# The second mixture's weights: loaded in the attention's last part instead of in the second routing

## The chip, the cores and the metric

One core of a Trainium2 chip runs the whole kernel. The metric is the device time of one execution in microseconds (us); lower is better. Fine effects are read in the profile of one execution, whose clock starts at its first instruction. The engines are named as in the profile: PE (TensorE, matrix products), PEld (its weight loads), DVE (VectorE), ACT (ScalarE), POOL (GpSimd), SP (SyncE, which here only issues DMAs).

## The reference

A sequence of 2048 tokens with 128 channels goes through three residual steps: a mixture of experts with half weight, an attention block, and the same mixture again, with the same weights.

```
x = x + 0.5 * mixture(layernorm(x))
x = x + attention_block(layernorm(x))
x = x + 0.5 * mixture(layernorm(x))
```

The mixture has eight experts, and each token goes to the two with the largest gate probability:

```
probs = softmax(x @ gate_W);  rw, sel = top_k(probs, 2);  rw = rw / rw.sum()
mlp_out = gelu(x @ mlp_W1 + b1) @ mlp_W2 + b2                 # experts 0 to 3, hidden 512
h0 = layernorm(x) * g0 + b0;   basis0 = 1 - tanh((h0 - grid) / 2)**2      # experts 4 to 7
z  = basis0 @ kan_W0 + c0      # 128 channels x 8 grid points -> 256
h1 = layernorm(z) * g1 + b1;   basis1 = 1 - tanh((h1 - grid) / 2)**2
kan_out = basis1 @ kan_W1 + c1 # 256 x 8 -> 128
out = sum over the two chosen experts of rw * expert_out
```

The attention block has 16 heads of 8 channels, a window of the 128 tokens before each one, and a gated feed-forward part with 352 hidden channels.

## The kernel before, in words

The kernel is written without a scheduler: every engine has its own list of instructions, and semaphores tie the lists together. A stage is a `nc.Block`; all five engines meet at a barrier at its end. The stages follow each other as

1. first routing (`route`, n = 0), 0 to 44 us,
2. first mixture (`moe_blocks`), to about 225 us, then the weighted sums into `xs`,
3. attention: `project`, `attend`, and `finish_attention` (the output product, the second layer norm and the feed-forward part), the last of them from 392 to 442 us,
4. second routing (`route`, n = 1), 442 to about 476 us,
5. second mixture (`moe_blocks`), to the end at 671.8 us.

**Routing.** VectorE normalizes the 16 tiles of 128 tokens (L307), TensorE transposes them (L496) and multiplies by the gate (L508). VectorE finds the two largest logits, counts the tokens of each expert, and builds tables that say for every block of 128 places which token rows it takes (L327 to L433). SP stores the normalized rows to memory in HBM (`x_rows`, L454) and a second copy of them, rescaled on ScalarE for the KAN experts (L534, store L457). At the end GpSimd gathers the rows of the first blocks with indirect DMAs (L477): `m_x_in` of the first MLP block, `k_x_in` of the first KAN block, `m_x_in` of the second MLP block. They wait for both stores (`rows_in_dram`) and for the tables (`rows_ready`).

**Mixture.** The number of blocks of each expert is known only at run time, so the engines read counts and expert numbers from tables into registers (L631, L558) and loop. TensorE begins with the transpositions of the first MLP block (L807) and the first KAN block (L829), then multiplies the MLP block by its expert's first weights (L813), which ScalarE has copied into `m_w1` (L1129). The first KAN product comes some blocks later (L835) and waits for all KAN weights.

**Weights.** `moe_weights` (L138) takes memory for one mixture's weights: 2 MB for both layers of the MLP experts, 0.25 MB for their biases, 8 MB for the KAN experts. In the kernel before it is called by `moe` for each mixture anew, and the memory is given back after the mixture; the attention lies in the same place. So SP loads the same weights twice, each time inside the routing: `load_mlps` (L163) and `load_kan` (L170), in one queue with the two stores of the rows. [...] In `finish_attention` SP has nothing to do.

Of the kernel before, what the change touches and what calls it, by code (L numbers as in the profile page):

```python
# [29 lines left out]
E2 = NE // 2  # L30
# [107 lines left out]
def moe_weights(nc, k, ctx, n):  # L138

    sb = lambda name, shape, dt=F32: ctx.enter_context(nc.sbuf_tensor(f"{name}_{n}", shape, dt))  # L140
    k.m_x_in = [sb(f"m_x_in{u}", [P, C]) for u in range(2)]
    k.k_x_in = sb("k_x_in", [P, C])
    k.rows_first = sb("k_rows_first", [P, 3, 1], I32)
    k.m_loaded = [k.sem(f"m_loaded{u}_{n}") for u in range(2)]
    k.k_loaded = k.sem(f"k_loaded_{n}")
    k.kan_w0 = sb("kan_w0", [P, E2, G, F2])
    k.kan_w1 = sb("kan_w1", [P, E2, F2C, G, C])
    k.mlp_w1 = sb("mlp_w1", [P, E2, F])
    k.mlp_w2 = sb("mlp_w2", [P, E2, FC, C])
    k.mlp_b2 = sb("mlp_b2", [P, E2, C])  # L150


def load_shared(q, k, a):

    q.dma_start(k.kan_ln[:], a.kan_ln).then_inc(k.small_loaded, 16)
    q.dma_start(k.kan_b0[:], a.kan_sl_b0.partition_broadcast(P)).then_inc(k.small_loaded, 16)
    q.dma_start(k.kan_b1[:], a.kan_sl_b1.partition_broadcast(P)).then_inc(k.small_loaded, 16)
# [5 lines left out]
def load_mlps(q, k, a, n):  # L163
    q.dma_start(k.mlp_w1[:], a.mlp_W1.rearrange("e p f -> p e f")).then_inc(k.mlp_loaded[n], 16)
    for e in range(E2):
        q.dma_start(k.mlp_w2[:, e], a.mlp_W2[e].rearrange("(c p) h -> p c h", p=P)).then_inc(k.mlp_loaded[n], 16)
    q.dma_start(k.mlp_b2[:], a.mlp_b2.partition_broadcast(P)).then_inc(k.mlp_loaded[n], 16)


def load_kan(q, k, a, n, e):  # L170
    q.dma_start(k.kan_w0[:, e], a.kan_sl_W0[e].rearrange("(p g) o -> p g o", g=G)
                ).then_inc(k.kans_loaded_again if n else k.kan_loaded[e], 16)
    q.dma_start(k.kan_w1[:, e], a.kan_sl_W1[e].rearrange("(c p g) o -> p c g o", p=P, g=G)
                ).then_inc(k.kans_loaded_again if n else k.kan_loaded[e], 16)
# [32 lines left out]
def route(nc, k, a, n, s):  # L207
# [6 lines left out]
    with ExitStack() as ctx:  # L214
# [13 lines left out]
        first = sb("first", [P, TOPK, NT])  # L228
# [51 lines left out]
        with nc.Block(no_gpsimd_drain=True) as block:  # L280
# [156 lines left out]
            @block.sync  # L437
            def _(sp):
                if n == 0:
                    x_tiles = a.x[0].rearrange("(t p) c -> p t c", p=P)  # L440
                    for g in range(NT // PART):
                        part = slice(g * PART, (g + 1) * PART)
                        sp.dma_start(k.xs[:, part], x_tiles[:, part]).then_inc(k.x_loaded[g], 16)
                    sp.dma_start(k.gate_w[:], a.gate_W).then_inc(k.gate_loaded, 16)
                    b1_rows = a.mlp_b1.rearrange("e (c p) -> (e c) p", p=P)
                    sp.dma_start(b1_rows_sb[:], b1_rows).then_inc(k.b1_loaded, 16)
                load_mlps(sp, k, a, n)
                if n == 0:
                    load_shared(sp, k, a)
                load_kan(sp, k, a, n, 0)  # L450

                rows = k.x_rows.rearrange("(h t p) c -> h p t c", h=2, p=P)
                sp.wait_ge(xn_ready, NT)
                sp.dma_start(rows[0], xn).then_inc(k.rows_in_dram[n], 16)  # L454
                load_kan(sp, k, a, n, 1)
                sp.wait_ge(xh_ready, NT)
                sp.dma_start(rows[1], xh).then_inc(k.rows_in_dram[n], 16)  # L457
                load_kan(sp, k, a, n, 2)
                load_kan(sp, k, a, n, 3)

            @block.gpsimd
            def _(pool):
# [752 lines left out]
                    sp.wait_ge(k.stored_out, 16 * (NT // PART))  # L1215


def moe(nc, k, a, n, s, out=None):

    with ExitStack() as ctx:  # L1220
        moe_weights(nc, k, ctx, n)
        route(nc, k, a, n, s)
        moe_blocks(nc, k, a, n, s, out)

NH = 16
HD = C // NH
PAIRS = NH // 2
# [475 lines left out]
def finish_attention(nc, k, a, s):  # L1703

    with ExitStack() as ctx:
# [28 lines left out]
        with nc.Block(no_gpsimd_drain=True) as block:  # L1734
            @block.tensor
            def _(pe):
# [28 lines left out]
                def by_w2(g):  # L1765
                    pe.wait_ge(hid_ready, 3 * g + 3)
                    if g < 2:
                        pe.wait_ge(h_ready, NCH)
                    else:
                        pe.wait_ge(x_ready, g - 1)  # L1770
                    for t in range(4):
                        for c, (at, size) in enumerate(HIDC):
                            last = nc.tensor.matmul(w_ps[g % 2][:, t], hid[g % 2][0:size, c, t * P:(t + 1) * P],
                                                    s.w2[0:size, c], start=(c == 0), stop=(c == 2))
                    last.then_inc(y_done, 1)
# [12 lines left out]
                    by_w2(g - 1)  # L1788
                by_w2(NCH - 1)

            @block.scalar
            def _(act):
                def affine(g):
                    act.wait_ge(nT_done, g + 1)
                    if g >= 2:
                        act.wait_ge(u_done, 3 * (g - 1))
                    nc.scalar.activation(n2T[g % 2][:], T_ps[g % 2][:], ACT.Identity, bias=s.ln_vec[:, 3:4],
                                         scale=s.ln_vec[:, 2:3]).then_inc(nT_ready, 1)

                act.preload_act_table(ACT.Silu)  # L1800
                def silu(g, c):
                    size = HIDC[c][1]
                    act.wait_ge(u_done, 3 * g + c + 1)
                    if g:
                        act.wait_ge(hid_ready, 3 * g + c - 2)
                    nc.scalar.activation(gate[0:size, c], u1_ps[(3 * g + c) % 2][0:size],
                                         ACT.Silu).then_inc(silu_done, 1)

                affine(0)
                silu(0, 0)  # L1810
                silu(0, 1)
                affine(1)
                silu(0, 2)
                for g in range(1, NCH):
                    if g + 1 < NCH:
                        affine(g + 1)
                    for c in range(3):
                        silu(g, c)
# [121 lines left out]
    return s  # L1940


def attention(nc, k, a, s):
    with ExitStack() as ctx:
        sb = lambda name, shape, dt=F32: ctx.enter_context(nc.sbuf_tensor(f"s_{name}", shape, dt))
        s.res = sb("res", [P, NT, C])
        s.mask_set = k.sem("mask_set")
        s.attT = sb("attT", [P, T])
        with ExitStack() as stacks:
            sb2 = lambda name, shape, dt=F32: stacks.enter_context(nc.sbuf_tensor(f"s_{name}", shape, dt))  # L1950
            s.qT = sb2("qT", [P, T + P])
            s.kT = sb2("kT", [P, T])
            s.q_bd = sb2("q_bd", [P, NB, HG, QB])
            s.k_bd = sb2("k_bd", [P, NB, HG, QB])
            s.v_bd = sb2("v_bd", [P, NB, NG, HG * HD])
            s.m_rows = sb2("m_rows", [P, T + P], BF16)
            s.mask = sb2("mask", [P, 2, P], BF16)
            s.no_keys = sb2("no_keys", [P, WINDOW], BF16)
            s.v_heads = sb2("v_heads", [P, NB, NG, HD])
            project(nc, k, a, s)  # L1960
            attend(nc, k, a, s)
        finish_attention(nc, k, a, s)

def macaron(nc, a, out):
    with ExitStack() as ctx:
        k = Names()
        k.sb = lambda name, shape, dt=F32: ctx.enter_context(nc.sbuf_tensor(name, shape, dt))
        k.sem = lambda name: ctx.enter_context(nc.semaphore(name))
        k.moe_sems = {}

        def moe_sem(name):
            if name not in k.moe_sems:
                k.moe_sems[name] = k.sem(name)
            return k.moe_sems[name]

        k.moe_sem = moe_sem
        k.x_rows = nc.dram_tensor("x_rows", [2 * T, C], F32, kind="Internal").ap()
        k.y_rows = nc.dram_tensor("y_rows", [ROWS_OUT, C], F32, kind="Internal").ap()
        k.xs = k.sb("xs", [P, NT, C])

        k.st = k.sb("st", [P, NT, 6])
        k.mv = k.sb("mv", [P, NT, 2])
        k.var_eps = k.sb("var_eps", [P, NT])
        k.rstd = k.sb("rstd", [P, NT])
        k.got = k.sb("got", [P, TOPK, NT, C])
        constants(nc, k)
        moe_tensors(nc, k)
        with ExitStack() as weights:
            s = attention_weights(nc, k, weights)
            moe(nc, k, a, 0, s)  # L1990
            attention(nc, k, a, s)
        moe(nc, k, a, 1, None, out)


# [40 lines left out]
```

## Time and profile before

| | |
|---|---|
| device time, median of 3 runs | 672.86 us (672.86 to 674.57) |
| the profiled execution | 673.61 us, its span 671.8 us |
| TensorE busy | 539.7 us, 80% of the span |
| VectorE busy | 450.6 us, 67% |
| ScalarE busy | 373.9 us, 56% |
| GpSimd busy | 263.3 us, 39% |
| mean granted TensorE clock | 0.903 |
| DMA | 46.51 MB, mean 69 GB/s |

The busy shares are means over stages of different kinds. TensorE's share says that it is the busiest, not that it sets the end everywhere. The chain of waits, followed back from the last instruction, and the windows show which stage waits for what. The line that matters for DMA is the row of slices: the DMA engines are nearly full in the first three slices (first routing) and in slices 27 to 29 (second routing), and nearly empty in the attention's last part.

### The profile page before, as it was taken

Reading aid. Unit: us, or ns where it says so; the run is one execution under the profiler, and the core shown is the slowest. Engines: PE = TensorE matmul, PEld = TensorE weight load, DVE = VectorE, ACT = ScalarE, POOL = GpSimd, SP = SyncE. Lnnn points to the kernel's source line nnn. Section 1 sums busy time; section 2 is a strip of 40 time slices with the busy share of each in tenths; the row PEclk is TensorE's granted clock in tenths of the full one; section 3 lists DMA queues with packets and bytes.
Section 4 is the critical chain, followed back from the end, with each engine's and each line's share of the span. In section 5 each row is a group of like instructions: output and inputs, shape, how many; then the busy total and the mean of one; then the engine's idle time right before and its main releaser. Section 6 shows DMA issues by size and latency. Waiting matters only on the chain. (4 is left out here: it accounts for less than half of the span.)

```text
span 671.8 us, 18348 instructions
## 1 busy us (share of the span) xinstructions
PE 539.7 (80%) x6060; PEld 469.2 (70%) x6061; DVE 450.6 (67%) x1166; ACT 373.9 (56%) x876; POOL 263.3 (39%) x305
## 2 busy tenths in 40 slices
PE   5248999999997368666999969972489999999960
PEld 4238899999986334554788855662378999999960
DVE  6744878877877488799133365548448688887855
ACT  2335889888944026600565512232368789888930
POOL 6035466666534255800000011120355566666430
PEclk9999999999999669797799978965599999999985
DMA  8972222100100300000000000069610000101106
GB/s 241 370 293 75 65 70 71 31 27 27 28 12 16 114 25 3 2 13 1 15 5 4 4 1 1 1 197 345 247 37 25 27 27 28 31 27 27 24 16 191
DMA packets 41235, 46.51 MB, mean 69 GB/s; under 512 B 7216, under 2 KB 33184, under 8 KB 40160
## 3 DMA queue, kind: packets, MB, share of 16 engines
q1 hardware_dynamic: 32224, 34.00, 15.5%
q0 software_dynamic: 4736, 9.71, 5.2%
q10 hardware_dynamic: 4224, 2.10, 1.0%
q8 instruction: 35, 0.57, 0.3%
q14 instruction: 16, 0.13, 0.1%
HBM read 35.69 MB, written 10.09 MB: 68 GB/s over the span
## 5 line engine op out<-in xcount | busy, mean ns | idle before, releaser
L845 PE MATMUL k_y_ps<-kan_w,k_basis 128*128 x1056 | 128.2, 281 | 8.2 <-DVE k_basis L941 6.6
L845 PEld LDWEIGHTS k_y_ps<-kan_w,k_basis 128*128 128x128 f32 x1056 | 124.6, 197 | 10.1 <-issue 9.8
L835 PE MATMUL k_z_ps<-kan_w,k_basis 128*128 x528 | 119.9, 380 | 1.2 <-issue 1.2
L1107 ACT ACTIVATE k_sig<-k_h1T 128x256 f32<-128x256 f32 x264 | 84.5, 402 | 52.9 <-DVE k_h1T L966 52.6
L835 PEld LDWEIGHTS k_z_ps<-kan_w,k_basis 128*128 128x128 f32 x528 | 97.7, 190 | 13.8 <-issue 1.6
L941 DVE SCALAR_TENSOR_TENSOR k_basis<-k_sig 128x512 f32<-128x512 f32 x132 | 85.9, 692 | 16.1 <-ACT k_sig L1107 16.1
L1100 ACT ACTIVATE k_sig<-k_h0T 128x128 f32<-128x128 f32 x280 | 59.2, 294 | 5.4 <-DVE k_h0T L929 5.4
L1670 ACT ACTIVATE got<-p_ps 128x960 f32<-128x960 f32 (+1 forms) x44 | 39.2, 944 | 27.4 <-PE p_ps L1586 27.4
L661 POOL DMA_INDIRECT y_rows<-k_y,k_rows x33 | 33.1, 1003 | 49.9 <-DVE k_y L973 32.0
L1634 DVE TENSOR_REDUCE p_minus_max<-p_ps 128x6 f32<-128x960 f32 (+1 forms) x44 | 46.0, 1117 | 5.0 <-PE p_ps L1551 4.7
L813 PE MATMUL m_z_ps<-m_xT,m_w 128*128 128x128 f32 x304 | 45.1, 296 | 4.9 <-DVE m_xT L979 2.2
L813 PEld LDWEIGHTS m_z_ps<-m_xT,m_w 128*128 128x128 f32 x304 | 43.1, 209 | 8.3 <-ACT m_w L1129 4.6
L1640 DVE RECIPROCAL p_inv<-p_ps 128x256 f32<-128x256 f32 x8 | 14.1, 1758 | 51.4 <-PE p_ps L1604 51.4
L935 DVE SCALAR_TENSOR_TENSOR k_basis<-k_sig 128x512 f32<-128x512 f32 x70 | 47.8, 685 | 0.0
L1536 PE MATMUL p_ps<-s_kT,s_q_bd 32*128 32x160 f32 (+4 forms) x512 | 30.4, 378 | 15.3 <-DVE p_minus_max L1634 11.4
L822 PE MATMUL m_y_ps<-mlp_w,m_hT 128*128 x304 | 41.7, 282 | 0.0
L1536 PEld LDWEIGHTS p_ps<-s_kT,s_q_bd 32*128 32x128 f32 x512 | 24.0, 236 | 21.7 <-DVE p_minus_max L1634 17.6
L822 PEld LDWEIGHTS m_y_ps<-mlp_w,m_hT 128*128 128x128 f32 x304 | 38.5, 199 | 0.0
L656 POOL DMA_INDIRECT k_x_in<-x_rows,k_rows x31 | 34.1, 1099 | 10.3 <-issue 8.8
L656 POOL DMA_INDIRECT j_x_in<-x_rows,j_rows x24 | 29.8, 1240 | 21.0 <-POOL j_rows L759 16.6
L1824 POOL TENSOR_TENSOR f_rstd<-f_var_eps,minus_half 128x4 f32<-128x4 f32 x4 | 5.5, 1383 | 80.6 <-DVE f_var_eps L1856 80.6
L668 POOL TENSOR_TENSOR k_rstd<-k_var_eps,minus_half 128x1 f32<-128x1 f32 x33 | 21.8, 659 | 39.1 <-DVE k_var_eps L956 39.0
(252 smaller groups left out, 1041.8 us busy)
## 6 DMA issues: line engine op xcount, KB each, us to landing
kan_w<-in_L_ffn_kan_sl_W_dram SPq DMA_DIRECT2D x16, 1024.0 KB, 10.0
x_rows<-got SPq DMA_DIRECT2D x4, 1024.0 KB, 12.0
mlp_w<-in_L_ffn_mlp_W_dram SPq DMA_DIRECT2D x2, 1024.0 KB, 5.7
mlp_w<-in_L_ffn_mlp_W_dram SPq DMA_DIRECT2D x8, 256.0 KB, 6.5
got<-y_rows SPq DMA_DIRECT2D x8, 256.0 KB, 4.9
got<-y_rows ACTq DMA_DIRECT2D x8, 256.0 KB, 5.3
xs<-in_L_attn_x_dram SPq DMA_DIRECT2D x4, 256.0 KB, 3.6
s_cos<-in_cos_dram SPq DMA_DIRECT2D x8, 128.0 KB
```

The costliest lines, as they stand in the source:

```text
L656: pool.indirect_dma_start(dst[:], None, k.x_rows, bass.IndirectOffsetOnAxis(ap=rows.bitcast(U32), axis=0)).then_inc(landed, 16)
L813: last = nc.tensor.matmul(m_z_ps[:, c], m_w1[:, c * P:(c + 1) * P], m_xT[:], start=True, stop=True)
L822: last = nc.tensor.matmul(m_y_ps, m_hT[:, c], k.mlp_w2[:, bass.ds(e, 1), c], start=(c == 0), stop=(c == FC - 1))
L835: last = nc.tensor.matmul(z_ps, basis0[:, g], k.kan_w0[:, bass.ds(e, 1), g], start=(g == 0), stop=(g == G - 1))
L845: last = nc.tensor.matmul(y_ps, basis1[:, g, c], k.kan_w1[:, bass.ds(e, 1), c, g], start=(g == 0 and c == 0), stop=(g == G - 1 and c == F2 ...
L935: nc.vector.scalar_tensor_tensor(basis0[:, part], sig0[:, part], 1.0, sig0[:, part], ALU.subtract, ALU.mult).then_inc(basis0_ready, 1)
L941: nc.vector.scalar_tensor_tensor(basis1[:, part], sig1[:, part], 1.0, sig1[:, part], ALU.subtract, ALU.mult).then_inc(basis1_ready, 1)
L1100: ins = nc.scalar.activation(sig0[:, g], h0T[:], ACT.Sigmoid, bias=float(-GRID[g]))
L1107: ins = nc.scalar.activation(sig1[:, g], h1T[:], ACT.Sigmoid, bias=float(-GRID[g]))
L1536: nc.tensor.matmul(banks[g][:, i * SPAN + lead:(i + 1) * SPAN], s.q_bd[rows(g), b], s.kT[rows(g), b * QB + lead - WINDOW:(b + 1) * QB], st ...
L1634: nc.vector.tensor_reduce(minus_max[:, h, 2 * half:2 * half + 2, b0:b0 + n], src, AX.X, ALU.max, negate=True).then_inc(reduced, 1)
L1670: nc.scalar.activation(prob[t % 2][:, 2 * half:2 * half + 2, 0:n * SPAN], ps[:, at:end, 0:n * SPAN], ACT.Exp).then_inc(exp_done, 1)
```

## The change

`moe_weights` for the second mixture is called after `attend` and before `finish_attention`, so the weights have their memory from there on (the memory of q, k, v and the masks is free by then). SP loads them in `finish_attention`. The routing for n = 1 keeps only its two stores on SP. `moe` and `attention` are taken apart and put together accordingly; the first mixture is as it was.

```diff
 # route(), SP's list
-                load_mlps(sp, k, a, n)
                 if n == 0:
+                    load_mlps(sp, k, a, n)
                     load_shared(sp, k, a)
-                load_kan(sp, k, a, n, 0)
+                    load_kan(sp, k, a, n, 0)
                 ...
                 sp.dma_start(rows[0], xn).then_inc(k.rows_in_dram[n], 16)
-                load_kan(sp, k, a, n, 1)
+                if n == 0:
+                    load_kan(sp, k, a, n, 1)
                 sp.wait_ge(xh_ready, NT)
                 sp.dma_start(rows[1], xh).then_inc(k.rows_in_dram[n], 16)
-                load_kan(sp, k, a, n, 2)
-                load_kan(sp, k, a, n, 3)
+                if n == 0:
+                    load_kan(sp, k, a, n, 2)
+                    load_kan(sp, k, a, n, 3)
 # finish_attention()
+            @block.sync
+            def _(sp):
+                load_mlps(sp, k, a, 1)
+                for e in range(E2):
+                    load_kan(sp, k, a, 1, e)
+
 # attention() becomes attention_and_mixture()
             project(nc, k, a, s)
             attend(nc, k, a, s)
+        moe_weights(nc, k, ctx, 1)
         finish_attention(nc, k, a, s)
+        route(nc, k, a, 1, None)
+        moe_blocks(nc, k, a, 1, None, out)
```

What SP does, before: the end of `attend`, then the whole list of the second routing (of `kan_w_1` the first three experts here; `finish_attention` has no row of its own).

```order
L1524 UNCONDITIONAL_BRANCH [waits p_m_loaded1,p_m_loaded0]
L437 UNCONDITIONAL_BRANCH [waits barrier_Pool_Activation_PE_DVE_SP_release]
L164 DMA mlp_w_1<-in_L_ffn_mlp_W_dram 128x4x512
L166 DMA mlp_w_1<-in_L_ffn_mlp_W_dram 128x4x128 x4
L167 DMA mlp_b_1<-in_L_ffn_mlp_b_dram 128x512
L171 DMA kan_w_1<-in_L_ffn_kan_sl_W_dram 128x2048
L173 DMA kan_w_1<-in_L_ffn_kan_sl_W_dram 128x2x1024
L454 DMA x_rows<-got 128x16x128 [waits xn_ready]
L171 DMA kan_w_1<-in_L_ffn_kan_sl_W_dram 128x2048
L173 DMA kan_w_1<-in_L_ffn_kan_sl_W_dram 128x2x1024
L457 DMA x_rows<-got 128x16x128 [waits xh_ready]
L171 DMA kan_w_1<-in_L_ffn_kan_sl_W_dram 128x2048
```

The first store stood behind eight loads, those of the MLP experts and of the first KAN expert, the second behind two more. SP's list in `finish_attention` now, up to the first KAN expert (three more pairs of L171 and L173 follow):

```order
L1519 UNCONDITIONAL_BRANCH [waits p_m_loaded1,p_m_loaded0]
L1786 UNCONDITIONAL_BRANCH [waits barrier_Pool_Activation_PE_DVE_SP_release]
L164 DMA mlp_w_1<-in_L_ffn_mlp_W_dram 128x4x512
L166 DMA mlp_w_1<-in_L_ffn_mlp_W_dram 128x4x128 x4
L167 DMA mlp_b_1<-in_L_ffn_mlp_b_dram 128x512
L171 DMA kan_w_1<-in_L_ffn_kan_sl_W_dram 128x2048
L173 DMA kan_w_1<-in_L_ffn_kan_sl_W_dram 128x2x1024
```

All 14 loads come right after the barrier at the end of `attend`, with no wait among them. SP's list in the second routing now:

```order
L1729 UNCONDITIONAL_BRANCH
L437 UNCONDITIONAL_BRANCH [waits barrier_Pool_Activation_PE_DVE_SP_release]
L454 DMA x_rows<-got 128x16x128 [waits xn_ready]
L458 DMA x_rows<-got 128x16x128 [waits xh_ready]
L280 UNCONDITIONAL_BRANCH
```

Only the stores are left, each behind its own wait. The instructions of the other four engines, their order and their waits are as before.

## Rows read from the trace of the kernel before

**Rows 1.** Windows: length, busy us and count per engine, PEclk, DMA share, GB/s

```profile
392.00:442.00 50.00, 43.50 (x192) 28.43 (x192) 31.23 (x112) 11.44 (x17) 9.56 (x8) 0.87 0.00 1
442.00:481.00 39.00, 18.08 (x87) 15.99 (x87) 23.05 (x98) 12.29 (x27) 5.85 (x4) 0.50 0.98 335
```

**Rows 2.** Timeline of SP in the second routing: start us, us, issue

```profile
442.32 0.40 SPq L164 DMA_DIRECT2D mlp_w<-in_L_ffn_mlp_W_dram  x1
...
458.88 0.47 SPq L457 DMA_DIRECT2D x_rows<-got  x1
...
468.49 0.43 SPq L173 DMA_DIRECT2D kan_w<-in_L_ffn_kan_sl_W_dram  x1
```

**Rows 3.** Chain of waits, 474 to 482 us: start us, us, what

```profile
474.42 0.18 DVE k_rows_first L420
474.60 0.46 issue
475.06 5.59 DMA m_x_in<-x_rows,rows_of
```

**Rows 4.** Timeline of TensorE; in brackets the idle time before and its releaser

```profile
480.69 0.48 PE L807 MATMUL m_xT_ps<-ident,m_x_in 128*128 128x128 f32 x1 [8.00 <-DMA m_x_in<-x_rows,rows_of]
481.05 0.47 PE L829 MATMUL k_xT_ps<-ident,k_x_in 128*128 128x128 f32 x1
...
486.93 1.91 PE L822 MATMUL m_y_ps<-mlp_w,m_hT 128*128 x8
...
490.35 1.06 PE L822 MATMUL m_y_ps<-mlp_w,m_hT 128*128 x8
```

**Rows 5.** Timeline of GpSimd: issues of the second and third gather

```profile
476.42 0.95 POOL L477 DMA_INDIRECT k_x_in<-x_rows,k_rows_first  x1 [0.30 <-POOLq L280]
477.68 0.94 POOL L477 DMA_INDIRECT m_x_in<-x_rows,rows_of  x1 [0.31 <-issue]
```

**Rows 6.** DMA issues, windows at 475.0, 476.4, 477.7, 481.4, 482.7: last number, us to landing

```profile
m_x_in<-x_rows,rows_of POOLq DMA_INDIRECT x1, 5.6
k_x_in<-x_rows,k_rows_first POOLq DMA_INDIRECT x1, 4.6
m_x_in<-x_rows,rows_of POOLq DMA_INDIRECT x1, 3.5
m_x_in<-x_rows,rows_of POOLq DMA_INDIRECT x1, 2.4
k_x_in<-x_rows,k_rows_first POOLq DMA_INDIRECT x1, 2.6
```

**Rows 7.** Timeline of ScalarE

```profile
450.49 4.78 ACT L534 ACTIVATE got<-got,rstd 128x128 f32<-128x128 f32 x16
...
478.22 0.62 ACT L1129 COPY m_w<-mlp_w 128x512 f32 x1
...
484.03 0.62 ACT L1129 COPY m_w<-mlp_w 128x512 f32 x1 [0.16 <-PE m_xT_ps L807]
```

**Rows 8.** Lines L631 and L558, VectorE's register reads: ns min/median/max, first and last start

```profile
L631 DVEq TENSOR_LOAD <-n_rounds x2: 352/352/352, 42.2 to 476.6; - x2
...
L558 DVEq TENSOR_LOAD <-experts x67: 308/544/981, 42.6 to 643.8; - x67
```

**Rows 9.** Line L457, the store of the rescaled rows, both routings

```profile
DMA to landing us min/median/max: 11.0/11.3/11.6
```

**Rows 10.** DMA queues: program fetches in 392:442, then 442:481 (packets, MB, share)

```profile
q8 instruction: 2, 0.03, 0.2%
...
q14 instruction: 1, 0.01, 0.0%
```

**Rows 11.** Windows at the clock's rises, columns as in rows 1

```profile
396.00:398.00 2.00, 1.92 (x10) 1.62 (x9) 1.93 (x8) 0.00 (x0) 1.39 (x1) 0.51 0.00 0
398.00:400.00 2.00, 0.91 (x8) 0.72 (x7) 1.93 (x11) 0.00 (x0) 0.87 (x1) 1.00 0.00 0
...
490.00:492.00 2.00, 1.50 (x13) 1.33 (x13) 1.18 (x3) 1.08 (x2) 1.53 (x2) 0.97 0.11 35
```

More of the change, by code:

```diff
@@ L1215, in _ @@
                     sp.wait_ge(k.stored_out, 16 * (NT // PART))
[L1218 to L1223, printed above, removed]
 NH = 16
@@ L1940, in attention_weights, with attention_and_mixture @@
     return s
-def attention(nc, k, a, s):
+def attention_and_mixture(nc, k, a, s, out):
     with ExitStack() as ctx:
@@ L1989, in macaron @@
             s = attention_weights(nc, k, weights)
-            moe(nc, k, a, 0, s)
-            attention(nc, k, a, s)
-        moe(nc, k, a, 1, None, out)
+            with ExitStack() as first:
+                moe_weights(nc, k, first, 0)
+                route(nc, k, a, 0, s)
+                moe_blocks(nc, k, a, 0, s, None)
+            attention_and_mixture(nc, k, a, s, out)
 _INS = ["L0_attn_x", "L0_attn_wq", "L0_attn_wk", "L0_attn_wv", "L0_attn_wo", "L0_attn_w1", "L0_attn_w2",
```

## The prediction, made before the changed kernel ran

> **What bounds the kernel now.** No engine is busy for the whole span, so each stage is judged by what it waits for. The change touches two, the attention's last part (392 to 442 us) and the second routing (442 to 481 us), and I took their windows first: the last part runs with the DMA engines empty (share 0.00), the second routing with them full (0.98, 335 GB/s) [rows 1]. Then SP's own rows: the first weight load of the second mixture goes out at 442.32, the last at 468.49, and the store of the rescaled rows at 458.88 stands between them [rows 2]. Then the chain of waits [rows 3]. From 442 to 474 it runs through TensorE and VectorE by turns (logits, top two, counting, the table of rows) without a DMA; the first one in it is the gather of the first MLP block's rows, issued at 475.06 after k_rows_first, 5.59 us long. TensorE's rows say the same from the other side: 8.00 us idle for m_x_in, then the transpositions of the first MLP block (480.69) and the first KAN block (481.05), then products [rows 4]. So what the weights can cost in the second routing is the landing of these gathers, and nothing ahead of them.
>
> **The change, part by part.**
>
> *Loads taken out of the second routing.* Three gathers are issued one behind the other, at 475.06, 476.42 and 477.68 [rows 3, 5]. They land after 5.6, 4.6 and 3.5 us [rows 6]: at 480.7, 481.0 and 481.2. Three durations, one common end, and that is where the DMA engines run empty. The next two, on empty DMA engines, land after 2.4 (m_x_in) and 2.6 us (k_x_in) [rows 6]; I take these for the first three once the weights are gone. The MLP block's rows then land at 475.06 + 2.4 = 477.5, the KAN block's at 476.42 + 2.6 = 479.0. TensorE takes both transpositions before the first product, so the later one decides: k_xT_ps starts near 479.0 in place of 481.05, and the product follows as now. Gain 4.6 - 2.6 = 2.0 us. From the first gather alone it would be 5.6 - 2.4 = 3.2 us; 1.2 of them are lost, since the second gather's issue doesn't move. The third lands near 480.3 and is wanted at about 481.5, after the first product: no wait. Bounds of this term: 0 and 3.2 us.
>
> What could be late in its place: ScalarE's copy of the first expert's m_w, 478.22 to 478.84 [rows 7], and VectorE, which has to read its round counts (0.35 us) and two rows of experts (0.54 us each, 0.98 at most) after the barrier at 476.5 [rows 8], before it copies m_xT. That gives 478.0, at worst 478.8. Both are ahead of 479.0, but by 0.2 to 1 us only; it is the step with least room. A copy of m_xT that begins at 478.8 and takes 0.3 us still loses nothing, since TensorE is at k_xT_ps until 479.5 (0.47 us).
>
> The Trainium skill (DMA: Bandwidth & Descriptors, Latency and other measured facts) says that an access to HBM takes 0.2 us on average and 2 us at high load. By that rule the KAN gather would get back 1.8 us, and the sum would be -1.8 us. The trace agrees in direction and gives 2.0.
>
> *The stores of the rows.* They lose the weights in front of them on SP. The second goes out at 458.88 now, 3.6 us after ScalarE's last rescaled tile (450.49 + 4.78 = 455.27) [rows 2, 7], and would go at about 455.3. The gathers wait for it, but today it lands at most 11.6 us after its issue [rows 9], by 470.5, and the table of rows is ready only at 474.4. Gain 0.
>
> *The loads put into the attention's last part.* 14 issues on SP, 10.25 MB: 32 us at 335 GB/s, from 392 to about 424, and the part ends at 442, so 18 us of room. SP has nothing else there, and no engine waits for SP before the barrier at 442. Nothing in that part reads what is loaded. Do full DMA engines slow the others? ScalarE's copy of m_w takes 0.62 us at 478.22, beside the weights, and 0.62 us at 484.03, after them [rows 7]: 0 us. What does share the DMA engines is each engine's program; two transfers of queue q8 (0.03 MB) fall in the last part and one of q14 in the second routing, beside the weights [rows 10]. Bounds: 0 us if the program stays ahead of its engine, and 5.6 - 2.4 = 3.2 us for each time that an engine stands for it, the price that a gather pays beside weights. I take 0: the one fetch in the second routing left no stand in the chain.
>
> The Trainium skill (Runtime: NRT & Kernel Launch, Instruction fetch mechanics) says that the next piece of program is fetched while the present one executes, and that only a taken branch to a place outside the pieces held makes an engine stand. By that rule the straight code of the last part costs 0 us and its entry is the one place to look at. No row of before shows a fetch beside loads in this part.
>
> *Memory and waits.* The second mixture's weights lie where q, k, v and the masks were, which are done with at the barrier before 392. No instruction is added on a computing engine, and no wait.
>
> **TensorE's clock.** It is at half (0.50, 1.2 GHz) through the second routing [rows 1] and at full (2.4 GHz) from about 490 [rows 11]. TensorE had begun again at 480.7, so the clock rose some 9.4 us later; in the attention's last part it rose 6 us after the start at 392.0 (0.51 until 398, then 1.00) [rows 11]. Eight passes of m_y_ps take 1.91 us at half clock and 1.06 at full [rows 4], so where TensorE sets the pace each us at half clock costs about 0.45. If the rise keeps its distance from the start, all moves by 2.0 us and the clock adds nothing; this I take. If it comes 6 us after the start, 3.4 x 0.45 = 1.5 us more are won; if it stays at 490, 2.0 x 0.45 = 0.9 are lost.
>
> **The sum.** -2.0 (gather) + 0 (stores) + 0 (last part) + 0 (clock) = -2.0 us. The profiled execution took 673.61 us (671.8 of span, 1.8 around it) and would take 671.6. It is 0.75 us above the median of the runs, 672.86 (two at 672.86, one at 674.57), and the forecast is made for the median: 672.86 - 2.0 = 670.8 us.
>
> **The rivals.**
> 1. *The clock rises sooner after the start.* -2.0 - 1.5 = -3.5: 669.3 us. For it: 6 us at 392. Against: 9.4 at 480.7, in the very stage.
> 2. *Another wait takes the gather's place*, VectorE's register reads or ScalarE's copy, or the clock's rise stays at 490. Then 0.5 to 1.1 us are left: 671.8 to 672.4 us. For it: the small room found above. Against: m_w is ready at 478.84 in the present trace.
> 3. *Slower.* The weights hold up a program fetch of TensorE or VectorE in the attention's last part. TensorE is busy there for 43.5 of 50 us [rows 1], in turn with VectorE, so a stand goes to the end nearly whole, and it decides once it exceeds the 2.0 us won. One stand: -2.0 + 3.2 = +1.2, 674.1 us; two: +4.4, 677.3 us. For it: fetches do fall there. Against: the second routing's showed no stand.
> 4. *It doesn't do what it says*: the loads are not through when the routing begins. They would have to run at 215 GB/s (10.25 MB in 50 us) where the trace has 335; then part of the gathers' wait stays, as in rival 2.
>
> **How the numbers follow.** Forecast case 0.50, rival 1 0.16, rival 2 0.25, rival 3 0.08, rival 4 0.01. What a measurement of this kernel can tell from no change is about 0.3%, here 2.0 us, and the forecast stands on that edge; I give a little over half of its case to the side beyond, because the profiled clock rose late. Faster by over 0.3%: 0.30 + 0.16 = 0.46. Slower by over 0.3%: rival 3 with two stands, 0.05. Within: 0.49. The range leaves out rival 3 and the far end of rival 1: 669.2 to 672.8 us.
>
> **What would show it.** In the profile after: DMA share near 1 from 392 to about 424 and near 0 from 465 to 475; the three gathers of the second routing at 2.4 to 2.7 us each; k_xT_ps 4.4 us after the end of k_rows_first, not 6.4; the attention's last part as long as now, and no new idle time with a queue of its own as releaser in it. The prediction is wrong if a gather still takes over 4 us, if TensorE's first product waits for ScalarE or VectorE, or if the last part has grown.

## The result, and the profile after

| | before | after |
|---|---|---|
| device time, median of 9 | 673.32 us (671.88 to 675.35) | 670.56 us (667.68 to 672.11) |
| the profiled execution | 673.61 us, span 671.8 | 667.68 us, span 665.9 |

The ratio is 0.9937, with a 95% interval of 0.9915 to 0.9959: 4.2 us faster, between 2.8 and 5.7. The means of the nine executions differ by 3.4 us, the medians by 2.8. The time is 0.24 us under the forecast of 670.8. But the forecast started from 672.86, and over nine executions the median of the kernel before is 673.32, 0.46 us higher; from there the sum gives 671.3. The gain is larger than the 2.0 us of the sum.

First the windows of the changed kernel, the attention's last part and the second routing (length, busy us and count of PE, PEld, DVE, ACT and POOL, PEclk, DMA share, GB/s):

```profile
390.10:440.90 50.80, 43.42 (x192) 28.41 (x193) 31.69 (x114) 11.42 (x17) 9.56 (x8) 0.87 0.58 212
442.00:478.00 36.00, 18.27 (x89) 16.18 (x89) 22.16 (x95) 12.28 (x27) 6.80 (x5) 0.50 0.21 64
```

The DMA share went from 0.00 to 0.58 in the first and from 0.98 to 0.21 in the second [rows 1]. PE's 43.42 us and 0.87 in the last part are those of before (43.50 and 0.87): what was put there lies beside other work. SP's timeline (start us, us, issue):

```profile
390.09 0.40 SPq L164 DMA_DIRECT2D mlp_w<-in_L_ffn_mlp_W_dram  x1
...
399.93 1.70 SPq L173 DMA_DIRECT2D kan_w<-in_L_ffn_kan_sl_W_dram  x1
444.63 0.38 SPq L454 DMA_DIRECT2D x_rows<-got  x1
453.33 0.37 SPq L458 DMA_DIRECT2D x_rows<-got  x1
```

All loads are issued in the first 11.5 us of the last part. The second store goes out at 453.33, as soon as its rows are rescaled, no longer 3.6 us behind them [rows 2, 7]. The chain of waits shows where that counts (start us, us, what):

```profile
474.42 0.04 issue
474.47 2.38 DMA k_x_in<-x_rows,k_rows_first
476.85 0.04 issue
476.89 0.48 PE k_xT_ps L831
477.37 1.83 PE m_z_ps L815 x8
```

The 5.59 us of the MLP block's gather [rows 3] have left the chain, and the KAN block's gather stands in it with 2.38. GpSimd's timeline has the three issues, 1.36 and 1.26 us apart as before [rows 5], and TensorE's what followed (in brackets the idle time before and its releaser):

```profile
473.10 1.06 POOL L479 DMA_INDIRECT m_x_in<-x_rows,rows_of  x1 [25.02 <-DVE k_rows_first L420]
474.47 0.95 POOL L479 DMA_INDIRECT k_x_in<-x_rows,k_rows_first  x1 [0.31 <-POOLq L280]
475.73 0.94 POOL L479 DMA_INDIRECT m_x_in<-x_rows,rows_of  x1 [0.30 <-issue]
```

```profile
475.68 0.48 PE L809 MATMUL m_xT_ps<-ident,m_x_in 128*128 128x128 f32 x1 [4.93 <-DMA m_x_in<-x_rows,rows_of]
476.89 0.48 PE L831 MATMUL k_xT_ps<-ident,k_x_in 128*128 128x128 f32 x1 [0.73 <-DMA k_x_in<-x_rows,k_rows_first]
477.16 2.03 PE L815 MATMUL m_z_ps<-m_xT,m_w 128*128 128x128 f32 x8
```

TensorE's idle time is 4.93 + 0.73 us, where it was 8.00 [rows 4]. From the first gather's issue to k_xT_ps it took 481.05 - 475.06 = 5.99 us before and 476.89 - 473.10 = 3.79 now: 2.20 us, where 2.0 were forecast. The gain at the first product is larger. These two lines are of the kernel before, VectorE's copy of the transposed MLP rows and the first product:

```profile
481.21 0.29 DVE L979 COPY m_xT<-m_xT_ps 128x128 f32<-128x128 f32 x1 [4.98 <-PE m_xT_ps L807]
481.65 2.04 PE L813 MATMUL m_z_ps<-m_xT,m_w 128*128 128x128 f32 x8
```

The MLP block's gather landed so late there that this copy ended at 481.50, and the product came 0.60 us behind the start of k_xT_ps. In the kernel after it comes 0.27 us behind it. From the first gather's issue to the first product it took 6.59 us before and 4.06 now, 2.53 us less. Neither ScalarE's m_w nor a register read holds it up. The clock kept its distance too: its rise shows here.

```profile
484.00:486.00 2.00, 2.00 (x17) 2.00 (x17) 0.65 (x3) 0.91 (x2) 0.69 (x2) 0.82 0.16 41
486.00:488.00 2.00, 0.95 (x9) 0.79 (x8) 0.82 (x2) 0.97 (x2) 1.66 (x2) 1.00 0.11 33
```

A mean of 0.82 in two us is 0.72 us at 0.50 and the rest at 1.00, so it rose at 484.7, 9.0 us after m_xT_ps; before it was some 9.4 [rows 11].

The profiled executions are 5.9 us apart, and 2.53 of that are the gathers' up to the first product. Of the rest, 1.65 us lie in the first mixture, 0.26 in the attention and 1.40 in the later second mixture, all code that is unchanged. One such place shows what these are. A stretch of the second mixture, first of the kernel before, then at the same place of the one after (columns as in the windows above):

```profile
647.00:651.00 4.00, 3.58 (x18) 3.59 (x19) 2.11 (x4) 1.39 (x5) 1.90 (x2) 0.57 0.10 33
```

```profile
641.00:645.00 4.00, 1.89 (x17) 1.90 (x18) 3.21 (x7) 2.56 (x8) 2.94 (x3) 1.00 0.06 19
```

The clock fell to half there in one execution and not in the other. A single pair of profiles therefore can't give the gain; the stage from the gather to the first product can be read in it, the sum can't. (Of e_defer_first below, one execution of 678.31 us in a slower state of the chip is left out.)

### The profile page after: what moved, and what is told of

The parts are those of the page before. It is cut to its first block and busy times, and to the rows that moved or that the text cites. A ratio compares the mean times of both kernels' runs of the same rounds, so it can differ in the third digit from the quotient of the medians.

```text
span 665.9 us, 18348 instructions
## 1 busy us (share of the span) xinstructions
PE 537.5 (81%) x6060; PEld 467.3 (70%) x6061; DVE 450.3 (68%) x1166; ACT 373.8 (56%) x876; POOL 264.4 (40%) x305
## 5 line engine op out<-in xcount | busy, mean ns | idle before, releaser
L847 PE MATMUL k_y_ps<-kan_w,k_basis 128*128 x1056 | 125.7, 278 | 7.9 <-DVE k_basis L943 6.3
L847 PEld LDWEIGHTS k_y_ps<-kan_w,k_basis 128*128 128x128 f32 x1056 | 122.3, 194 | 9.7 <-issue 9.5
```

The lines of the kernel that those rows point to most:

```text
L847: last = nc.tensor.matmul(y_ps, basis1[:, g, c], k.kan_w1[:, bass.ds(e, 1), c, g], start=(g == 0 and c == 0), stop=(g == G - 1 and c == F2 ...
```

## The experiments

In all of them the counts read at run time are kept at 1 or more by a register instruction; c_before and c_after are the two kernels with that alone, and are what the others are compared with.

```diff
-                k.n_rounds[0:1, :], engines=[eng.engine], min_val=1, max_val=NS,
+                k.n_rounds[0:1, :], engines=[eng.engine], min_val=0, max_val=NS,
...
+            found = [smax(v, 1) for v in found]
```

Times are means of 12 executions (6 for e_late_9us and e_defer_second, 11 for e_defer_first, 13 for e_warm_after), ratios are to the kernel before on the same chip, with 95% intervals. The chips differ: the kernel before takes 679.4 and 679.2 us (medians) on the chip of c_before, c_after, e_mlps_only and e_twice and on that of e_again, e_product_first and the two warm kernels, and 673.5 and 673.8 on the two of the others. The second of these chips has no control of its own; there only ratios are compared with the controls. Only one chip's times are subtracted from each other. "g1 to k_xT" is the time from the first gather's issue to k_xT_ps in the profile.

### Three pairs: how large is the gain?

Both controls were run three times (_2 and _3 are the same kernels on other chips).

> The kernel before, with one register operation more for each of the four round counts (a lower bound of 1), which changes no count. It is the partner of c_after. Every theory: same as before within 0.3%. Its profile is a second drawing of the same program: if the 2.0 us by which the changed kernel's profile was already ahead at 390 us (unchanged code) is chance of the clock, the second routing should begin anywhere between 439 and 444 us here; if it belongs to the change, it begins at 442.4 again.

> The changed kernel with the same lower bound on the round counts. Theory A (the gathers alone): 2.0 to 2.2 us under c_before, ratio to before 0.997; the rest of the first measurement (0.9937, 4.2 us) was chance of TensorE's clock in stages that the change doesn't touch. Theory B (something else is won too, in the clock or in the last part): again 3.5 to 4.5 us, ratio 0.994.

> c_before again, for a second set of runs and a third drawing of the kernel before's profile. Every theory: 1.002 of before. The KAN gather of the second routing beside weights took 4.6, 5.3, 5.2 and 6.5 us so far; here again 4.6 to 6.5.

> c_after again. Theory A (the gathers are the whole gain, 2.2 to 2.8 us in the profiles): with both sets of runs together the pair's difference settles at 2.2 to 3.2 us. Theory B: it stays at 3.8 us or more, above what the gathers' landing can give.

> c_before again, as the common partner of the next three on one chip. Every theory: 1.0015 of before, KAN gather 4.6 to 6.5 us. Theory C (besides 2.5 us of landing, about 1 us comes from TensorE's clock): its runs spend 3 to 6 us more at half clock than c_after_3's.

> c_after again. Theory A (landing alone): 2.5 us under c_before_3. Theory C (landing and clock): 3.2 to 3.8 us under it, 0.996 of before, with 3 to 6 us less at half clock, of which the shorter wait itself is 2.5.

| pair | ratio of c_before | ratio of c_after | difference of means | g1 to k_xT |
|---|---|---|---|---|
| 1 | 1.0021 [0.9995, 1.0046] | 0.9968 [0.9943, 0.9994] | 681.02 - 677.86 = 3.2 us | 6.68, 3.98: 2.70 |
| 2 | 1.0013 [0.9994, 1.0032] | 0.9963 [0.9945, 0.9980] | 674.76 - 671.51 = 3.3 us | 6.45, 3.93: 2.52 |
| 3 | 1.0028 [1.0004, 1.0051] | 0.9959 [0.9942, 0.9976] | 675.50 - 671.60 = 3.9 us | 6.71, 3.90: 2.81 |

Weighted, the time's difference is 3.4 us, plus or minus 0.75 if all executions are taken as independent, and 3.4 is also what the means of before and after give. By the ratios the three differences are 3.6, 3.4 and 4.6 us, and their intervals are wider. The stage's is 2.7, to k_xT_ps and to the first product alike. The second routing's first transposition came at 441.1 to 445.4 us in the three profiles of c_before and at 444.4 to 445.3 in those of c_after, so the 2 us by which the first profile of the changed kernel was ahead there were chance. The chain of c_before names what it is:

```profile
479.02 5.28 DMA k_x_in<-x_rows,k_rows_first
484.30 0.04 issue
484.34 0.49 PE k_xT_ps L831
```

The KAN gather took 5.28 us here, 5.05 in c_before_2 and 5.30 in c_before_3, where the kernel before had 4.6 [rows 6]; without the weights it took 2.44, 2.53 and 2.48.

### Part of the change: only the MLP weights moved

```diff
 # finish_attention(), SP
                 load_mlps(sp, k, a, 1)
-                for e in range(E2):
-                    load_kan(sp, k, a, 1, e)
 # route(): the four load_kan stand where they stood before the change, for both n
```

> The changed kernel with only the MLP experts' 2.25 MB loaded in the attention's last part; the KAN experts' 8 MB stay in the second routing, in the old places on SP. 10 MB (weights and stores) at 335 GB/s take 31 us from 442, so the DMA engines are empty near 473, 2 us ahead of the gathers. Theory A (only a gather beside weights costs): the gathers land in 2.4 to 2.7 us and the whole gain is there, as c_after. Rival (loads in the routing cost in proportion, or their presence slows the routing): a fifth to a quarter of the gain, 0.5 to 1 us.

677.04 us, 0.9958 [0.9931, 0.9984]: 0.8 us under c_after, within its noise, and 4.0 under c_before. As far as these runs can tell, the whole gain comes with 2.25 of the 10.25 MB. Windows of e_mlps_only (columns as above):

```profile
460.00:473.00 13.00, 4.43 (x22) 3.75 (x23) 10.91 (x47) 1.78 (x2) 0.00 (x0) 0.50 1.05 394
473.00:475.00 2.00, 2.00 (x13) 1.67 (x12) 1.43 (x6) 0.00 (x0) 0.00 (x0) 0.50 0.64 258
475.00:484.00 9.00, 3.20 (x15) 2.40 (x14) 3.68 (x18) 2.65 (x7) 4.37 (x5) 0.50 0.08 24
```

The 8 MB of KAN weights are through by about 474.3, and the KAN gather goes out at 479.78 and lands after 2.41 us. What counts is not how much is loaded in the routing but whether it is through when the gathers go out.

### Does a loaded last part cost anything?

Here SP loads the KAN weights twice in the attention's last part, and the first KAN product waits for both copies.

```diff
                 for e in range(E2):
                     load_kan(sp, k, a, 1, e)
+                sp.wait_ge(k.kans_loaded_again, 16 * 2 * E2)
+                for e in range(E2):
+                    load_kan(sp, k, a, 1, e)
```

> The changed kernel with the KAN experts' 8 MB loaded a second time behind the first, 18.25 MB in all: the DMA engines stay full from 390 through the whole of the attention's last part, to about 445. Theory A: no effect on that part (49 us from its first product to its last xs) and none on the gathers; time as c_after within 0.3%. Rival (loads beside that part cost it through program fetches or memory): the part grows, by up to 3 us.

```profile
395.00:444.00 49.00, 43.61 (x192) 28.46 (x192) 31.24 (x112) 11.43 (x17) 8.55 (x8) 0.87 0.92 350
```

676.76 us, 0.9957 [0.9928, 0.9986], no slower than c_after. With the DMA engines at 0.92 through the part (0.58 in after) PE's 43.61 us are as before (43.50), and from the part's first product to the second routing's first transposition it took 50.88 us, before 50.83. Rival 3's price is 0 here, for a part into which two transfers of queue q8 and one of q14 fall (0.04 MB). The Trainium skill (Runtime: NRT & Kernel Launch, Instruction fetch mechanics) says that straight code has its next piece fetched while the present one runs; this run agrees.

### The same traffic beside the gathers

All weights come early as in c_after, and the KAN weights are then loaded once more behind the second store of the second routing. Only traffic is added. The first KAN product now waits for the late copy too, but that is through at about 482 and the product starts at 500.34.

```diff
 # route(), SP, behind the second store
+                else:
+                    for e in range(E2):
+                        load_kan(sp, k, a, n, e)
```

> c_after with the KAN experts' 8 MB loaded a second time, in the second routing behind the second store, so that the DMA engines are full when the three gathers go out, as before the change; everything else of the change stays (memory, first loads in the attention's last part). Theory A (gathers beside weights are the whole gain): the KAN gather takes 4.6 to 5.3 us again and the time is c_before's, 681.0 us on that chip, that is 1.002 of before. Theory B (about 1 us of the 3.8 between c_before and c_after's kind comes from elsewhere in the change): 1 us less, 0.9995 to 1.001 of before. The load ends some 5 us later than before the change (8 MB from 456 on take 24 us, with the stores), and TensorE waits for the KAN weights at 499, so no wait there.

```profile
477.89 5.16 DMA k_x_in<-x_rows,k_rows_first
483.05 0.04 issue
483.09 0.49 PE k_xT_ps L836
```

679.97 us, 1.0012 [0.9990, 1.0034]: the gain is gone, and the gather takes 5.16 us. The DMA share is 1.00 until 482 and 0.05 in the 2 us behind it, so no later transfer of the mixture has weights beside it. So the transfers beside the gathers are the cause. The memory's new place, the shorter list of SP and the earlier stores aren't, but for a part that this interval can't see: Theory B's 1 us lies in it.

### Is a later start worth as much as it is long?

GpSimd does idle work before the first gather of the second routing, in the kernel after: one operation in e_late_3us, three in e_late_9us.

```diff
                 pool.wait_ge(rows_ready, 1)
+                if n:
+                    for i in range(IDLE):
+                        nc.gpsimd.tensor_tensor(idle[i][:], var_eps2[:], k.minus_half[:], ALU.pow)
```

> c_after with the first gather of the second routing held back by one idle GpSimd operation (rstd of 128x16, 2.9 us in the profile before), and empty DMA engines. It puts a delay of the size of the slow gathers where they were, with nothing on the DMA queues. Theory A: +2.9 us on c_after_3, us for us. Theory C (a later start of the mixture costs more than its length, because TensorE's clock is low for longer): +3.5 to +4.3 us, and 4 to 6 us more at half clock. Rival D (the missing 1 us comes from the traffic itself, not from the lateness): +2.9 here, and c_before_3 stays 3.4 or more above c_after_3.

> The same with three idle operations, 8.7 us. Theory A and rival D: +8.7 us. Theory C with a cost in proportion: +10.5 to +12.5; with a fixed cost (a longer idle time of TensorE lets the clock's rise come later by a constant): +9.3 to +10.3.

GpSimd's timelines, first of e_late_3us, then of e_late_9us:

```profile
473.21 2.90 POOL L489 TENSOR_TENSOR idle<-var_eps,minus_half 128x16 f32<-128x16 f32 x1 [24.38 <-DVEq L421]
476.29 1.06 POOL L481 DMA_INDIRECT m_x_in<-x_rows,rows_of  x1 [0.17 <-issue]
```

```profile
476.21 8.63 POOL L489 TENSOR_TENSOR idle<-var_eps,minus_half 128x16 f32<-128x16 f32 x3 [24.34 <-DVEq L421]
485.01 1.06 POOL L481 DMA_INDIRECT m_x_in<-x_rows,rows_of  x1 [0.17 <-issue]
```

From the first transposition of the routing to the first gather's issue it took 34.64 and 40.32 us, c_after_3 32.22: the delays are 2.42 and 8.10 us, and g1 to k_xT stays at 3.87 and 3.86. The times are 674.20 (0.9999 [0.9973, 1.0025]) and 681.10 (1.0094 [1.0066, 1.0123]), so 2.6 and 9.5 us above c_after_3; by the ratios 2.7 and 9.1. That is 1.1 to 1.2 us for each us of delay, but the 2.6 are plus or minus 1.4 and the 9.5 plus or minus 1.6, so the longer delay leaves 1.0 to 1.4, and one for one isn't excluded. So the runs don't decide between Theories A and C. The clock's rise kept its distance, 8.5 and 9.8 us after m_xT_ps where c_after_3 had 7.6. By the best estimate the 2.7 us of the stage are worth some 3.0 to 3.2 us of time, against 3.4 plus or minus 0.75 measured. A second effect of the change (rival D) isn't needed, and one of about 1 us isn't excluded: c_before_3 lies 3.9 us above c_after_3 and 1.3 plus or minus 1.8 above e_late_3us, whose delay is 0.4 us shorter.

### Can the clock be kept up?

TensorE does idle products at the end of the last part and at three waits of the second routing.

```diff
+KEEP = (3, 4, 5, 3)
+                def keep(times):
+                    if n:
+                        for _ in range(times):
+                            nc.tensor.matmul(xT_ps[0][:], k.ident[:], xnT[:, 0:4 * P], start=True, stop=True)
+                keep(KEEP[1])
                 pe.wait_ge(up_to_ready, 1)
```

> c_before with idle products on TensorE that keep its clock up: 3 at the end of the attention's last part, and 4, 5 and 3 in the waits of the second routing, all 512 columns wide into memory that nothing reads. Every theory: TensorE stays at full clock from 442 on, the logits' chain shrinks from 10.4 us by about 4 and the mixture's start by 3 to 4, so 6 to 8 us under c_before. It is the partner of e_warm_after; alone it tells what the low clock costs.

> The same idle products in c_after. Theory A: the difference to e_warm_before is the gathers' landing alone; with the routing 4 us shorter the weights of e_warm_before end even later against the gathers, so 2.8 to 5 us. Theory B (a part of the gain is the clock's, which rises sooner when the mixture starts sooner): with the clock held, that part is gone and the difference is at the lower end, 2 to 3 us, under the 3.8 us of the pair without idle products.

679.18 us, 1.0005 [0.9986, 1.0024], and 676.05 us, 0.9954 [0.9936, 0.9972]. Windows of e_warm_before:

```profile
446.00:450.00 4.00, 4.00 (x26) 4.00 (x26) 2.40 (x11) 1.17 (x2) 1.45 (x1) 0.65 1.04 338
450.00:454.00 4.00, 4.00 (x19) 3.81 (x18) 0.45 (x2) 3.10 (x10) 1.45 (x1) 0.50 1.12 345
454.00:462.00 8.00, 8.00 (x20) 3.73 (x19) 6.55 (x33) 3.86 (x10) 0.00 (x0) 0.78 1.00 329
```

TensorE is busy without a gap and still gets 0.65, 0.50 and 0.78. From first transposition to first gather 30.67 and 30.65 us are left of 32.2: only 1.5 us sooner, where 3 to 4 were expected. The 6 to 8 us of the expectation didn't come: beside the controls on other chips the warm kernels gain next to nothing (before 1.0005 beside 1.0013 to 1.0028; after 0.9954 beside 0.9959 to 0.9968). But the pair is 3.1 us apart, in line with the others, with KAN gathers of 6.53 and 2.43 us. TensorE's work in the routing doesn't visibly touch what the change gives. It is no test with the clock held, since it wasn't held.

### Three other ways round the gather

*The MLP block's product before the KAN block's transposition*, in both mixtures, in the kernel after:

```diff
                 m_turn(m_x_in[0], m_loaded[0], 1)
-                turn(0)
                 pe.wait_ge(k.mlp_loaded[n], 16 * N_MLP)
                 pe.sem_inc(m_y_ready, 1)
                 by_w1(1)
+                turn(0)
```

> c_after with TensorE's first product ahead of the transposition of the first KAN block, so that it waits only for the MLP block's rows (2.4 us after 477.5) and for ScalarE's m_w. Theory A (the KAN gather, issued 1.4 us later, decides the start): the product starts 0.5 to 0.8 us sooner, since ScalarE's m_w is the next thing late, and VectorE's affine step of the KAN block comes later by the product's 2 us, which may take it back: -0.8 to +0.5 us to c_after. Rival: no change at all, because VectorE's register reads end only when the KAN rows are there.

681.54 us, 1.0032 [1.0009, 1.0054]: by the ratios 4.3 us slower than c_after, whose runs were on another chip. The chain, and behind it ScalarE's timeline, have the reason why the product can't come much sooner:

```profile
485.14 0.35 DVEq L634
485.49 0.03 issue
485.52 0.97 DVEq L561
486.49 0.03 issue
486.52 0.31 DVEq L561
486.83 0.05 issue
486.88 0.30 DVE m_xT L983
```

```profile
486.76 0.62 ACT L1133 COPY m_w<-mlp_w 128x512 f32 x1
```

VectorE's register reads after the barrier take 1.7 us and end at 486.83, just 0.06 us after m_xT_ps. Its copy of m_xT is done at 487.18, and ScalarE's m_w only at 487.38; the product starts at 487.44. So m_w is what it waits for last, by these times, though the chain names the copy of m_xT. The first product starts 3.8 us after the first gather's issue (4.3 in c_after), and the second 9.0 us after it (7.5), with VectorE's and TensorE's later steps in another order. This is the small room that the prediction spoke of: m_w is no bound as long as the product waits for the KAN gather, and is one as soon as it doesn't. To the first KAN product the stage is 1.6 us longer than in c_after. The edit changes both mixtures, and where the rest of the 4.3 us lies isn't shown.

*Weights put off into the mixture.* In e_defer_second the kernel before loads its KAN experts 2 and 3 only once the first gathers of the second mixture have landed; in e_defer_first the kernel after does that with expert 3 of the first mixture.

```diff
 # moe_blocks(), SP, n = 1 (e_defer_first: n = 0, expert 3)
+                    sp.wait_ge(turned, 1)
+                    sp.wait_ge(m_loaded[1], 16)
+                    load_kan(sp, k, a, n, 2)
+                    load_kan(sp, k, a, n, 3)
```

> c_before (weights' memory and loads as before the change) but the last two KAN experts' 4 MB of the second mixture are issued after the three first gathers have landed, in the mixture. Theory A: what counts is that the DMA engines are free at 477, so the KAN gather takes 2.4 to 2.7 us and most of c_after's gain is there, though no byte is loaded in the attention's last part. Against it stand the deferred 4 MB, on the way from 482 to 495: the next gathers are beside them, and TensorE wants all KAN weights at 496 to 499. 0.997 to 0.999 of before. Rival (the gain comes with the move into the last part): as c_before, 1.002.

> c_after, and in the first mixture the last KAN expert's 2 MB issued after the first three gathers have landed. It uses the same lever in the first routing, where the change left it: there the gathers at 40.6, 42.1 and 43.4 us land beside weights (5.1, 3.8 and 2.7 us), the second against 2.6 clean. Theory A: 1.2 us or a little more under c_after, 0.994 of before. Rival: the deferred load slows the next gathers by as much, no change.

e_defer_second took 676.83 us, 1.0047 [1.0031, 1.0062], slower than c_before_2 (1.0013), although its KAN gather took 2.54 us and g1 to k_xT 3.94. From k_xT_ps to the first KAN product it needed 20.0 us instead of 16.1. Its chain:

```profile
485.92 0.29 DVE m_y L997
486.21 0.80 issue
487.01 6.22 DMA y_rows<-m_y,m_rows
```

The scatter of a finished block's rows now runs beside the weights and takes 6.22 us, 2.61 in c_before_2. The wait was moved, not removed. e_defer_first came to 670.97 us, 0.9961 [0.9938, 0.9983], and c_after_2 to 671.51: 0.5 us less, plus or minus 1.6, so no gain is shown. Its stage did shrink: in the first routing g1 to k_xT took 4.12 us where c_after_2 has 6.85, and the first KAN product of the first mixture came at 61.16 in place of 63.81. A start 2.65 us sooner didn't show in the time there; what takes it back is open.

## Why the prediction came out short

*Loads taken out of the second routing: the mechanism was right, its size wrong, and this is the step that failed.* "The later one decides: k_xT_ps starts near 479.0 in place of 481.05" holds for the kernel after: the KAN gather stands in its chain, and e_again brings back both its length and the time. But the term 4.6 - 2.6 = 2.0 us was too small in two ways. The first could be read in the rows of before. That "the product follows as now" was wrong: in that execution it was the MLP block's late gather and the copy of m_xT behind it that held the first product to 481.65, 0.60 us behind k_xT_ps. With both gathers early that distance is 0.27 us, so the first product gained 2.53 us where k_xT_ps gained 2.20. The second is that both durations came from one execution. The gather beside weights took 4.6 us in that one and 5.05, 5.28, 5.30, 5.16 and 6.53 in c_before_2, c_before, c_before_3, e_again and e_warm_before: the execution at hand had the shortest. Without weights it took 2.3 to 2.5, and 2.6 was the upper end. The stage is worth 2.7 us by the three pairs. The bounds of 0 and 3.2 us held it.

The price of a wait was also put at one us of time for each us. The delays of 2.42 and 8.10 us cost 1.1 to 1.2 by their best estimate, and 1.0 isn't excluded. With 1.1 to 1.2 the stage makes about 3.1 us of the 3.4 measured. What of the last 0.3 is chance can't be told at an uncertainty of 0.75. The first ratio's 4.2 us drew somewhat high; its interval holds both 3.1 and 3.4, and just misses 2.7. The 2.0 of the sum lies outside of it. That the time came so near the forecast of 670.8 is luck in part: the base was 0.46 us higher than taken, and the gain larger.

*The page of the Trainium skill weighed there* (DMA: Bandwidth & Descriptors, Latency and other measured facts: 0.2 us on average, 2 us at high load) gave 1.8 us. The pairs show 2.7, so the measurement decides against it, as a size for a gather of 128 rows.

*The stores: 0, right.* The second went out 3.6 us sooner after its rows, and from first transposition to first gather both kernels took 32.19 us.

*The last part: 0, right*, and e_twice shows it with twice the KAN traffic. The working of it was off in two details without a price: the weights ran at 347 GB/s from 390 to 410 and faster behind it, and were through after 30 us rather than 32, and SP was done issuing after 11.5 us. Its list had been drawn out to 26 us before by the load right behind each store, whose issue took 8.90 and 8.08 us (most others 0.4 to 0.5); in the kernel after none took over 2.2 us.

*The clock: 0, right for the stage.* The rise came 9.0 us after m_xT_ps where before it was 9.4, and over all profiles with that stage alike between 7.6 and 11.0. Rival 1's 6 us were never seen. The price of 0.45 us for each us at half clock was taken from passes back to back; over whole executions it is 0.24 (below).

*Rival 2* (something else late) didn't occur in this order of work, and e_product_first shows that ScalarE's copy stands right behind, by 0.5 us. *Rival 3* isn't seen in e_twice, with more traffic than the change has. *Rival 4* is false by the windows of after.

*The chances.* Faster by over 0.3% was given 0.46 and happened. The case "within" got 0.49 because the one sum stood on the edge. Further executions put the gather's duration at 5.05 to 6.53 us, and a term of 2.7 would have given 670.2 us at 1 us for each, and most of the chance to faster. With one draw of a loaded transfer the term had a spread that the chances didn't carry.

## What to carry to other kernels

Look for small indirect transfers at a stage's start that run beside a bulk load, and move the bulk load only as far as needed for it to be through by then; here 2.25 of 10.25 MB gave all that could be measured. Follow the gain to the first instruction that needs all its inputs, since another late input may have stood just behind the one in view. Take a duration under load from several executions, or treat the one at hand as a draw: the gather on idle DMA engines repeated to 0.3 us, beside a full load it ranged over 1.9. Moving the load behind the first gathers handed the wait to the next small transfer in e_defer_second.

## What the runs showed of the hardware

- An indirect DMA of 128 rows (gather into k_x_in) takes 2.3 to 2.6 us on DMA engines with next to nothing else to do (after and the c_after runs, e_twice), and 4.6 to 6.5 us beside weights at 385 to 415 GB/s (before and the c_before runs, e_again, e_warm_before). A scatter of a block's rows took 2.61 us in c_before_2 and 6.22 in e_defer_second.
- TensorE, busy without a gap for 4 us at a time, was given a clock of 0.65 and 0.50 of full speed in e_warm_before. Being busy alone did not keep it up.
- Equal programs differ by where the clock falls. Over 189 executions of the 17 kernels other than the kernel before, compared within one kernel, each us more at half clock (worked out from span and mean clock) went with 0.24 us more of span, standard error 0.02.
- TensorE's busy time in the attention's last part is the same to 0.2 us at DMA shares of 0.00, 0.58 and 0.92 (43.50, 43.42, 43.61 us).
